# A decoder's cross-attention kernel: 16 of a pair's 24 blocks of probabilities transposed on four 32-row tiles of TensorE instead of two 64-row tiles

## The reference

```python
q_r = jnp.einsum('bshq,hqr->bhsr', q_big, W_qr)      # 8 x 16 heads x 56 tokens x 64
k_r = jnp.einsum('bld,hdr->bhlr', kv_r, W_kr)        # kv_r: the context, rotated, 8 x 1500 x 64
scores = jnp.einsum('bhsr,bhlr->bhsl', q_r, k_r)     # 8 x 16 x 56 x 1500
attn = jax.nn.softmax(scores, axis=-1)
ctx_c = jnp.einsum('bhsl,bld->bhsd', attn, kv_r)
ctx_lat = jnp.einsum('bhsd,hkd->bhsk', ctx_c, w_kc_kv)
return ctx_lat.transpose(0, 2, 1, 3).reshape(Bv, Sv, H * K) @ Wo.T
```

## Time and profile before

| | |
|---|---|
| median of 3 runs | 1669.82 us (1664.1 to 1678.85) |
| profiled execution | 1674.1 us, its span 1672.3 us |
| TensorE busy | 1629.8 us (97%), mean granted clock 0.989 |
| VectorE, ScalarE busy | 1112.3 us (67%), 750.0 us (45%) |
| matmuls of the turn, L1117 | 4032, busy 239.8 us |
| matmuls of weigh, L1130 | 4608, busy 240.5 us |
| matmuls of the scores, L1030 | 1008, busy 233.0 us |
| copies of the turn: ScalarE L1238, VectorE L1329 | 336 and 168, busy 172.5 and 107.6 us |

### The profile page before, as it was taken

One profiled execution on the slowest core, in us unless ns is written; L12 is line 12 of the kernel. 1 busy time (PEld: TensorE's weight loads), 2 busy tenths in 40 slices (PEclk: granted clock), 3 DMA queues, 4 the chain that ended last, 5 costly groups with the idle time before them and its releaser, 6 DMA issues.

```text
span 1672.3 us, 35626 instructions
## 1 busy us (share of the span) xinstructions
PE 1629.8 (97%) x15226; PEld 1107.3 (66%) x15226; DVE 1112.3 (67%) x1964; ACT 750.0 (45%) x1297; POOL 239.0 (14%) x428
## 2 busy tenths in 40 slices
PE   8999999999999989999999999999999999999998
PEld 5575367777755756655367777764566767777765
DVE  2825889999566753266889999535445289999633
ACT  2223366666412642144366666312444366666411
POOL 0011300000010312011200000010455000000030
PEclk9999999999999899999999999999999999999999
DMA  9212010000040011051020000050300220000010
GB/s 279 75 23 82 1 77 2 2 2 2 2 186 1 2 58 40 1 122 58 1 96 2 2 2 2 2 241 1 63 1 1 114 89 2 2 2 2 2 44 11
DMA packets 35494, 71.10 MB, mean 43 GB/s; under 512 B 25331, under 2 KB 29747, under 8 KB 31405
## 3 DMA queue, kind: packets, MB, share of 16 engines
q1 hardware_dynamic: 35338, 68.83, 12.6%
HBM read 68.36 MB, written 0.46 MB: 41 GB/s over the span
## 4 chain that ended last, share of the span: by engine, by line
PE 91%; DVE 5%; ACT 2%; issue 1%; DMA 1%; POOL 0%; DVEq 0%; SPq 0%; ACTq 0%; POOLq 0%
PE ps L1117 14%; PE ps L1130 14%; PE ps L1030 13%; PE ps L362 10%; PE ps L1491 9%; PE ps L941 3%; PE ps L2579 3%; PE ps L1145 3%; PE ps L524 2%; PE ps L1948 2%; PE ps L951 1%; PE ps L2606 1%; PE ps L170 1%; PE ps L977 1%; PE ps L962 1%
## 5 line engine op out<-in xcount | busy, mean ns | idle before, releaser
L1231 ACT ACTIVATE arena<-ps,softmax_stats 128x1500 f32<-128x1500 f32 x168 | 253.9, 1511 | 195.3 <-DVE softmax_stats L1312 193.2
L1130 PEld LDWEIGHTS ps<-arena,ctx_pos 125*64 125x64 f32 x4608 | 222.3, 137 | 58.4 <-issue 56.8
L1117 PE MATMUL ps<-ident,arena 64*125 64x64 f32 x4032 | 239.8, 272 | 1.9 <-ACT arena L1231 1.6
L1130 PE MATMUL ps<-arena,ctx_pos 125*64 125x128 f32 (+1 forms) x4608 | 240.5, 262 | 0.0
L1117 PEld LDWEIGHTS ps<-ident,arena 64*125 64x125 f32 x4032 | 227.3, 186 | 17.0 <-issue 13.5
L1030 PE MATMUL ps<-ctx_feat,arena 64*128 64x500 f32 x1008 | 233.0, 595 | 0.0
L1238 ACT COPY arena<-ps 125x512 f32<-125x512 f32 x336 | 172.5, 600 | 78.6 <-PE ps L1117 78.6
L1310 DVE TENSOR_REDUCE softmax_stats<-ps 128x1 f32<-128x500 f32 x252 | 170.6, 678 | 52.0 <-PE ps L1030 51.9
L362 PE MATMUL ps<-arena 128*128 128x256 f32 x736 | 174.5, 383 | 3.1 <-DVE arena L1618 1.3
L1323 DVE TENSOR_SCALAR arena<-arena,softmax_stats 128x1500 f32<-128x1500 f32 x168 | 168.3, 1002 | 5.9
L1491 PE MATMUL ps<-x_feat,arena 128*128 128x448 f32 (+1 forms) x416 | 167.9, 549 | 1.2 <-DVE arena L1601 1.2
(11 more groups left out here) (321 smaller groups left out, 1930.3 us busy)
## 6 DMA issues: line engine op xcount, KB each, us to landing
ctx_pos<-in_ctx SPq DMA_DIRECT2D x1, 2688.0 KB
arena<-in_L1f_gate SPq DMA_DIRECT2D x1, 2304.0 KB, 11.8
arena<-in_L1f_up SPq DMA_DIRECT2D x1, 2304.0 KB, 16.8
arena<-in_L1f_down SPq DMA_DIRECT2D x1, 2304.0 KB, 7.8
arena<-in_L0a_Wq SPq DMA_DIRECT2D x1, 2048.0 KB, 11.4
arena<-in_L0a_Wc SPq DMA_DIRECT2D x1, 2048.0 KB, 19.4
arena<-in_L0x_Wq SPq DMA_DIRECT2D x1, 2048.0 KB, 9.9
arena<-in_L0x_Wo SPq DMA_DIRECT2D x1, 2048.0 KB, 8.6
```

Source lines behind the costliest of these rows:

```text
L1117: m = nc.tensor.transpose(c.ps[0:LP, turn_bank(i, k, r), n * 64:(n + 1) * 64], probs[i % 2][e][rows, l * LP:(l + 1) * LP], c.ident[rows, r ...
L1130: m = nc.tensor.matmul(y[r * 64:(r + 1) * 64, lo:hi], c.ctx_pos[:, j, l, e, :], pT[i % 2][:, lo // 64:hi // 64, LT * e + l, :], start=(l = ...
L1231: nc.scalar.activation(probs[i % 2][e].rearrange("p (k l) -> p k l", k=3), sc[e], ACT.Exp, bias=low[:, i % 4, e:e + 1], accum_out=total[:, ...
```

## The change

Unit 0 of each stage is turned as before (`turn_first`, `copy_first`). For units 1 to 27 the new `turn(i)` has two parts:

- **Quarters.** The first 16 blocks (all 12 of e = 0, four of e = 1) are each turned in four instructions of 32 query rows instead of two of 64: 32 x 125 numbers are loaded as weights at row tile t, and a 32 x 32 identity is streamed. Tile t writes to bank `quarter_bank(i, t)`: 0, 1, 2, 7 (2, 3, 4, 7 for the last unit). All four banks fill over the whole part, and each is reported when its 16th block is done.
- **Halves.** The other eight blocks are turned as before on two 64-row tiles, into banks 6 and 5.

The six copies keep their number and size: VectorE copies quarters 0 and 1, ScalarE quarters 2 and 3 and then the two halves. A quarter's copy writes 16 runs of 32 numbers per partition instead of one run of 512.

```diff
+    def quarter_bank(i, n):
+        return ((2, 3, 4, 7) if i == NU - 1 else (0, 1, 2, 7))[n]
...
             if i > 1 and k == 2:
-                pe.wait_ge(a_in.handle, a_in.at(4 * (i - 2) + 3))
+                pe.wait_ge(a_in.handle, a_in.at(4 * (i - 2) + (2 if i == 2 else 3)))
...
-        def turn(i, k):
-            if k == turn_order(i)[0]:
-                for e in range(2):
-                    pe.wait_ge(normed[e].handle, normed[e].at(i + 1))
-            if k == 0 and i < NU - 1:
-                pe.wait_ge(exped[0].handle, exped[0].at(i + 2))
-            if k == 2 and i > 0:
-                pe.wait_ge(kept.handle, kept.at(i))
...
+        def turn(i):
+            for e in range(2):
+                pe.wait_ge(normed[e].handle, normed[e].at(i + 1))
+            if i < NU - 1:
+                pe.wait_ge(exped[0].handle, exped[0].at(i + 2))
+            for n in range(16):
+                e, l = divmod(n, LT)
+                for t in range(4):
+                    rows = slice(t * 32, (t + 1) * 32)
+                    m = nc.tensor.transpose(c.ps[0:LP, quarter_bank(i, t), n * 32:(n + 1) * 32],
+                                            probs[i % 2][e][rows, l * LP:(l + 1) * LP], c.ident[rows, rows],
+                                            tile_position=(t * 32, 0))
+                    if n == 15:
+                        m.then_inc(*turned_quarter[t].next())
+            pe.wait_ge(kept.handle, kept.at(i))
+            if i < NU - 1:
+                pe.wait_ge(exped[1].handle, exped[1].at(i + 2))
+            for n in range(8):
+                for r in range(2):
+                    rows = slice(r * 64, (r + 1) * 64)
+                    m = nc.tensor.transpose(c.ps[0:LP, half_bank(r), n * 64:(n + 1) * 64],
+                                            probs[i % 2][1][rows, (n + 4) * LP:(n + 5) * LP], c.ident[rows, rows])
...
+        def copy_quarter(i, n):    # ScalarE, n = 2, 3
+            act.wait_ge(turned_quarter[n].handle, turned_quarter[n].at(i))
+            nc.scalar.copy(pT[i % 2][:, n // 2, 0:16, n % 2 * 32:(n % 2 + 1) * 32],
+                           c.ps[0:LP, quarter_bank(i, n), :].rearrange("p (s q) -> p s q", s=16)).then_inc(*a_in.next())
...
+        def copy_quarter(i, n):    # VectorE, n = 0, 1
+            dve.wait_ge(turned_quarter[n].handle, turned_quarter[n].at(i))
+            nc.vector.tensor_copy(pT[i % 2][:, 0, 0:16, n * 32:(n + 1) * 32],
+                                  c.ps[0:LP, quarter_bank(i, n), :].rearrange("p (s q) -> p s q", s=16)).then_inc(*d_in.next())
```

83 lines of the change are left out of this document (50 added, 33 removed).

## The result

| | before | after |
|---|---|---|
| median | 1672.45 us (4 runs, 1664.1 to 1678.85) | 1709.39 us (4 runs, 1696.03 to 1719.23) |
| ratio, 95% interval | | 1.0207 [1.0165, 1.0249] |
| profiled execution, span | 1674.1, 1672.3 us | 1696.0, 1694.2 us |
| mean granted clock | 0.989 | 0.988; the other three 0.973, 0.983, 0.974 |

The change makes the kernel about 2% slower. The forecast was 1682 us, 0.75% slower, and the range ended at 1701: it was wrong, and too low.

The account below looks back on a forecast made before the run. TensorE, busy 97% of the span, was taken to bound the kernel. Terms of 10.5, 1.7 and 0.4 made 12.6 us; on the scale of the 1669.8 median the forecast was 1682 us, 0.75% slower, range 1658 to 1701.

Parts of the forecast that it names:

- What sets the speed of a transpose: In the turn: the weight load, not the stream of identity columns, sets the pace of 0.109 us a block.
- The rival in which the stream is the limit: Quarters' 16 blocks take 0.87 us less, of which 0.22 comes through in 78 turns; faster, 1650 us; chance 0.10.
- Cost 1, the quarters: First 16 blocks: four 32-row loads run together at 0.109 us a block, 1.75 us before and after; term 0.
- Cost 2, the change of shape: Between quarters and halves: the change from 32-row to 64-row tiles loses 0.14 us a turn; bounds 0 and 0.14.
- Cost 3, VectorE's copies: Behind the turn: copies start later, scores' load 0.12 us later beside the 0.14 gap; VectorE catches up; term 0.
- Cost 4, the ends of the stages: Projection behind unit 26's turn waits for both copies, 0.57 us a stage; unit 27's turn loses 0.14.
- The step that failed: Steady loop: any change in TensorE's turn moves the end equally, unless another engine makes TensorE wait.
- the loads did run together: Rival on the quarters: four loads go two at a time, 1.75 us more in 81 turns, 1824 us; chance 0.06.
- the one with VectorE: Rival: VectorE, 0.08 us to spare at the third maximum, doesn't catch up; 0.2 more in 78 turns, 1698; chance 0.21.
- the fourth: Rival: 32-row instructions land on 64-row tiles, time as before, or only late copies remain, 1681 us; chance 0.03.
- G: Follow-up theory on the steady loop: the clock falls when a turn streams little and has gaps on top.

Follow-up runs that it names:

- e4: Kernel before, each turn load taking 128 columns instead of 125 except for a row's last block; 1628.64 us, ratio 0.9729.
- e3: Kernel before, first 16 blocks of the turn each transposed in one instruction on the whole array, copies as early as before; 1680.46 us, ratio 1.0046.
- e9: e6 and e1 together: thin products on 64-row tiles and late VectorE copies, against the kernel before; 1715.27 us, ratio 1.0232.
- e14: e6 with e2's small 32-row matmul, so two more changes of tile shape, copies not late; 1795.59 us, ratio 1.0713.
- e6: Kernel before, first 16 blocks replaced: every second one as an ordinary two-pass product streaming 32 columns on 64-row tiles, others left out; 1671.17 us, ratio 0.9995.
- e13: e6 with one more ordinary product of 112 streamed columns per tile before the last eight blocks, lengthening the turn without a gap; 1686.34 us, ratio 1.0071.
- e1: Kernel before, VectorE's two copies waiting for the turn's 16th block instead of the eighth; 1684.05 us, ratio 1.0076.
- e2: Kernel before, one small matmul on a 32-row tile before the last eight blocks, so two more changes of shape; 1709.89 us, ratio 1.0232.
- e7: Changed kernel, quarters on tiles 0 and 2 alone except for the 16th block; 1755.99 us, ratio 1.0509 to the kernel before.
- e10: Kernel before, first 16 blocks on the lower 64-row tile alone except each eight's last block, with e1's late copies; 1688.3 us, ratio 1.0081.

## Why the prediction was wrong

- **What sets the speed of a transpose: right.** The load does. e4 shows it from the other side: quicker loads with the same stream make the turn quicker. The rival in which the stream is the limit (0.10) is out. One of the two arguments for the load was weak, though: L1506's matmuls last as long as the turn's with twice the stream, but their loads are the quick ones of 140 ns, which the profile before already showed. The Trainium skill, TensorE: Matmul & The Clock Gate, Weight-path perf modes, says that the fast weight load needs 128 weights and a type other than 32-bit float. For ordinary products the traces agree: 128 columns of 32-bit float take 187 ns (L1030). For transposes they agree on the 128 and not on the type (186 against 138 ns, in 32-bit float), and the measurement decides.
- **Cost 1, the quarters: right.** The 64 records take 1.94 us, a block (1.94 - 0.29) / 15 = 0.110, and four loads run together. One load for 32 rows takes 184 ns, one for 64 took 186:

```profile
L1134 PEld LDWEIGHTS ps<-ident,arena x5184: 178/184/184, 226.0 to 1600.8; 32*125 32x125 f32 x200
L1134 PE MATMUL ps<-ident,arena x5184: 268/268/291, 226.0 to 1600.8; 32*125 32x32 f32 x200
```

- **Cost 2, the change of shape: right.** The quarters end at 285.90 + 1.94 = 287.84, and the halves' load is at 287.76, 0.08 before. The halves begin 1.86 after the quarters, where 16 blocks at 0.109 are 1.74: 0.12 for the change of shape, where 0.14 was forecast. The turn is 2.80 from start to start instead of 2.67; the last 0.01 of that 0.13 is the wait for VectorE's first copy. The Trainium skill, TensorEngine Tiling, Key Properties, says that a change of the mode drains the engine; the trace agrees, and also between 64 and 32 rows.
- **Cost 3, VectorE's copies: nearly right.** They start 1.96 after the turn (forecast 2.00), and VectorE catches up before the next turn. But the step took TensorE's load to come 0.05 after a copy's end, and it came 0.12 after: the first copy ends at about 287.86 + 0.69 = 288.55, the load is at 288.67. With that wait the two tiles start apart, and the scores grew by 0.05, which the step did not have. The unit is 8.29 where 8.25 was forecast; at 75 turns that is 3 us. The timeline of the kernel after, in place of the earlier trace rows:

```profile
287.86 1.29 DVE L1378 COPY arena<-ps 125x512 f32<-125x512 f32 x2 [0.72 <-PE ps L1134]
287.93 1.07 ACT L1273 COPY arena<-ps 125x512 f32<-125x512 f32 x2 [0.60 <-PE ps L1134]
```

- **Cost 4, the ends of the stages: right.** The projection comes 442.56 - 439.26 = 3.30 after the turn's start, and came 2.76 after it: 0.54, forecast 0.57.

```profile
439.26 1.94 PE L1134 MATMUL ps<-ident,arena 32*125 32x32 f32 x64
441.12 1.08 PE L1145 MATMUL ps<-ident,arena 64*125 64x64 f32 x16
442.56 3.67 PE L1173 MATMUL ps<-arena 128*64 128x256 f32 x32 [0.36 <-DVE arena L1378]
```

- **The step that failed** stands in the first paragraph: in the steady loop "whatever lengthens or shortens TensorE's turn moves the end by as much". It took the granted clock for given. The sum had no term for it, and no rival did. The profile before shows 1.00 over a unit, and outside the loops it does show the clock at the lower level, so it could have been asked what the turn now gives the engine to do. The change halves what each block streams and adds gaps, and the loop, which had stood at full clock in all of its 72 units, began to fall to the lower one. That is 12 us in the profiled run and about 21 by the medians, more than one and a half times the whole sum of 12.6. e3, with the same unit and no falls, comes out at 1680, two microseconds from the forecast; that it comes so near is in part luck, since its clock outside the loops is better than before.
- **The rivals.** Of the two slower ones, VectorE was not late, and the loads did run together. The 1698 of the one with VectorE lies nearer the result than the forecast, by another road. The instructions did land on 32-row tiles (32*125 in the rows above), which ends the fourth. Every rival, as the sum, priced the unit alone.

That the falls come with a thin turn and gaps together is shown, by e9 and e14 against e6, e13, e1 and e2, within the limits said above on the length of the unit. Why the clock behaves so isn't. Open as well is why e7, with the same unit and two tiles, has 34 falls where four tiles have 7 and 11: G alone doesn't say how many. e10 adds to it: it has the gap, one tile at work instead of two, each block streamed in full, and no fall, so fewer tiles alone are not what thins the work in e9. How tiles and columns count together no run here tells.

## What to carry to other kernels

Before a tile shape is made smaller, find out whether the load or the stream sets the pace: if it is the load, a smaller stream gains nothing and only leaves the engine less to do. Where a loop runs TensorE at full clock, count the granted clock as a term of its own, and compare it unit by unit before and after; two edits that are free or cheap alone (e6 costs nothing, e1 0.8%) can cost 2.3% together. And look at the load's column count first where blocks are transposed: 128 instead of 125 made this kernel 2.7% faster, and the quarters then added nothing. For ordinary products no run here shows such a gain.

## What the runs showed of the hardware

- In a 32-bit transpose a weight load of 128 columns takes 138 ns on a 64-row tile where one of 125 takes 186, and the pace of pairs goes from 0.109 to 0.062 us. On 32-row tiles it is the same (64 records in 1.23 us instead of 1.94). In an ordinary 32-bit product 128 columns take 187 ns on 64-row tiles (L1030). The 96 columns of the earlier trace rows, such a product, paced at 0.085.
- The granted clock can fall on an engine that the records show busy without a break: 9.98 of 9.98 us in the unit that falls. In the unit ahead of it the longest times without a weight load are 0.2 us among the scores, 0.17 ahead of the turn and 0.74 ahead of weigh, the last as long in the kernel before, which has no falls. The Trainium skill, TensorE: Matmul & The Clock Gate, A second HAM failure mode, puts such swings down to short idle times between groups of matmuls. The trace agrees that gaps are needed (e6 none, e9 11 falls), and not that they are enough (e2 has the same gaps as e14, and 0 falls against 48).
- In the steady loops of all traces with falls, the clock fell between 0.25 us before and 0.8 us behind the start of the scores, and each slow unit cost 1.7 us (9.98 against 8.29; 10.25 against 8.55 in e14).
- Where the scores waited for VectorE's copy, the load came 0.12 us after the copy's end (0.05 in the earlier trace rows), and the two tiles of the product stayed 0.036 us apart instead of 0.003.
